# A two-layer decoder stack on one core: late recurrent outputs in the query bank of the next attention, and another order inside a recurrent step

## The chip, the core and the metric

The program runs on one core of a Trainium2 chip. Five engines work from their own instruction queues: TensorE (PE in the profile; its weight loads are the row PEld), VectorE (DVE), ScalarE (ACT), GpSimd (POOL) and SyncE (SP), which here only issues DMAs. An engine runs its instructions in the order in which they were written; engines wait for each other by semaphores. The metric is the device time of one execution in microseconds (us), and the median of several runs is compared.

## The reference

The input x has 2 sequences of 1024 rows and 256 columns, ctx two sequences of 154 rows and 192 columns, all float32. Six blocks are added to x one after the other, each on the layer norm of x:

```
x = x + L0_attn(norm(x)); x = x + L0_xattn(norm(x), ctx); x = x + L0_ffn(norm(x))
x = x + L1_attn(norm(x))          # the recurrent attention
x = x + L1_xattn(norm(x), ctx)    # 16 heads of 16 columns over 154 keys
x = x + L1_ffn(norm(x))           # 8 experts, the best 2 of each row
```

The change is about the fourth block and the beginning of the fifth. In the fourth, `bitlinear(x, w)` is an rms norm of the row, a rounding to integers by the row's largest value, and a product with weights of -1, 0 and 1:

```
i, f, g = bitlinear(x, w_i), sigmoid(bitlinear(x, w_f)), bitlinear(x, w_g)
h[n] = f[n] * h[n-1] + (1 - f[n]) * i[n]              # along the sequence
out  = bitlinear(rmsnorm(h) * g * sigmoid(g), w_o)
```

The fifth is an ordinary attention: queries `norm(x) @ Wq + bq`, softmax over the 154 keys for each of 16 heads, and an output product.

## The kernel before, in words

The 2048 rows are 16 tiles of 128 rows (`NT`); a pair is two tiles (`PAIR`), and there are 8.

**The recurrent stage** is `recurrent`. Each engine runs a loop over `STEPS = NT + LAG` = 29 steps k. In step k TensorE turns the rounded rows of tile k+1 (`turn`), multiplies those of tile k by the three gate weights (`products`), turns forget gate and new state of tile k-1 so that rows lie along the free axis (`scan_turn`), and turns the scanned state of tile k-2 back (`turn_back`). ScalarE makes the sigmoids, the copies and the sums of squares. VectorE scans (L2035, one scan for each half of the columns), multiplies the state that was turned back with the gate (`u`, L2022), makes the gate (L2042) and the new state (L2047), and in `ROW_STEPS` does the row work for tiles 8 to 15 (largest values, scales). GpSimd makes `1 - f` (`keep`, L1791), the gate times its norm (L1785), `zo` = u times its norm (L1796), and the rounding. The rounding of `zo` needs the scale of the row; these scales are made for many tiles at once (`out_scales`, at steps 10 and 18). The output of tile o (turn, copy, product, addition to x at L2052, statistics for the next layer norm at L133) runs in step o + 13, so that steps 16 to 28 hold no new gates, only outputs.

**The cross attention** is the class `CrossNarrow`. Some of it runs inside the recurrent steps, by `pool_step`, `tensor_step` and their like: its keys and values, the split of its weights into a high and a low part (L3464 to L3471, steps 15 to 17), the normalised tiles 0 to 3 (L3476, steps 19 and 20), and the queries of pair 0 (steps 21 to 24). The rest is `run`. There a tile goes through six groups of scores (L3801), their largest values (L3964), the exponentials (L3910), five turns of the probabilities (L3817, L3821; the fifth gets its rest from GpSimd's gather, L3781), the weighing of the values (L3835, L3838), and the output product (L3862). The queries of a pair go through the normalised rows (`normal`), their turn (`turn_x`, L3532), a high part (`high_x`, L3597) and a low part (`low_x`, L3627), 12 products (L3544), a high part (L3608) and a low part (L3634), and 12 DMAs that lay them out by heads (L3433: eight of `cn_qh`, four of `cn_ql`). The scores of a pair's first tile wait for these DMAs.

The order of all this on each engine is fixed before by `order`: a list of work items with an estimated span and the items they depend on is put in a sequence, always taking next the item that could start first by these estimates. The engines then run their part of that sequence.

## Time and profile before

| | |
|---|---|
| median of 3 runs | 1428.05 us (1425.85 to 1431.0) |
| the profiled execution | 1432.4 us, its span 1430.7 us |
| PE, PEld busy | 1296.7 us (91%), 1037.2 us (72%) |
| DVE busy | 1010.1 us (71%) |
| ACT busy | 882.9 us (62%) |
| POOL busy | 457.0 us (32%) |

The shares are means over six blocks with different limits. The profile gives times from the start of the span; the recurrent stage's first gate product starts at 818.38 us and the attention's first scores at 917.25 us. The granted clock is the share of TensorE's full 2.4 GHz that it was allowed in a stretch: 0.50 is 1.2 GHz. A wait is put down to the engine and the line that released it.

### The profile page before, as it was taken

To read this page: it belongs to the slowest core of one execution; us is meant where nothing else is said; L and a number is where in the kernel's file an instruction comes from. 1 tells how busy PE (TensorE), PEld (TensorE's weight loads), DVE (VectorE), ACT (ScalarE), POOL (GpSimd) and SP (SyncE) were. 2 spreads that over 40 slices of the span, in tenths; PEclk is the share of its full clock that TensorE was granted. 3 is DMA by queue.
4 is the path that set the end of the run, shared out by engine and by line. 5 is a ranking of instruction groups with operands and counts; after the bars stand their busy time and mean duration, and the time that the engine had idled before them with its cause. 6 is when DMAs were issued, how large, how long until landed. Compare 5 with 4: busy or idle time off the path is not lost. (4 is left out here: it accounts for less than half of the span.)

```text
span 1430.7 us, 27678 instructions
## 1 busy us (share of the span) xinstructions
PE 1296.7 (91%) x9691; PEld 1037.2 (72%) x9691; DVE 1010.1 (71%) x2014; ACT 882.9 (62%) x2215; POOL 457.0 (32%) x628
## 2 busy tenths in 40 slices
PE   4979999999699999989999866689988699999997
PEld 3534444436599999977888654578877699999995
DVE  4687878734566665556788687578875688888773
ACT  4427666774476666645121467478873688888883
POOL 5311222218444333326000356311100244444430
PEclk8979999999899999999999987599998799999998
DMA  4655422200000000003000210022203577777755
GB/s 91 189 122 138 68 46 47 47 1 5 30 2 2 1 2 1 2 6 121 1 0 1 75 24 1 23 62 47 51 10 107 187 232 232 232 233 233 230 158 188
DMA packets 97916, 116.15 MB, mean 81 GB/s; under 512 B 23549, under 2 KB 83187, under 8 KB 97779
## 3 DMA queue, kind: packets, MB, share of 16 engines
q1 hardware_dynamic: 88323, 99.83, 25.7%
q0 software_dynamic: 4416, 12.06, 2.6%
q10 hardware_dynamic: 5040, 2.49, 0.7%
q8 instruction: 78, 1.28, 0.4%
q14 instruction: 59, 0.48, 0.1%
HBM read 88.47 MB, written 16.55 MB: 73 GB/s over the span
## 5 line engine op out<-in xcount | busy, mean ns | idle before, releaser
L827 ACT ACTIVATE sa_probs<-ps 128x512 f32<-128x512 f32 (+1 forms) x304 | 154.5, 577 | 87.6 <-PE ps L780 86.4
L851 DVE TENSOR_REDUCE sa_top<-ps 128x2 f32<-128x1024 f32 (+3 forms) x160 | 171.8, 1114 | 40.9 <-PE ps L756 25.5
L2738 PE MATMUL ps<-me_h,me_w_parts 128*128 128x256 f32 x1104 | 140.9, 288 | 4.8 <-issue 2.9
L2738 PEld LDWEIGHTS ps<-me_h,me_w_parts 128*128 128x128 f32 x1104 | 137.3, 193 | 6.4 <-issue 3.1
L2752 PE MATMUL ps<-me_w_parts,me_mid 128*128 128x256 f32 x1104 | 136.3, 283 | 0.0
L2752 PEld LDWEIGHTS ps<-me_w_parts,me_mid 128*128 128x128 f32 x1104 | 132.4, 188 | 0.0
L3246 ACT ACTIVATE room<-ps,cx_top 128x154 f32<-128x154 f32 x256 | 96.6, 391 | 35.4 <-DVE cx_top L3295 34.9
L2819 DVE TENSOR_TENSOR me_w_parts<-me_chunk,me_w_parts 128x1024 fp32r<-128x1024 f32 x92 | 110.4, 1222 | 9.9 <-ACT me_w_parts L2779 8.3
L2803 ACT ACTIVATE me_full<-ps,me_b 128x256 f32<-128x256 f32 x184 | 95.2, 518 | 34.7 <-PE ps L2738 34.5
L2849 DVE TENSOR_TENSOR me_mid<-me_full,me_mid 128x256 fp32r<-128x256 f32 x184 | 89.9, 506 | 34.7 <-ACT me_mid L2805 34.6
L3125 POOL TENSOR_TENSOR room<-room 128x512 f32<-128x512 f32 x64 | 67.1, 1049 | 140.7 <-DVE room L3303 140.6
L753 PE MATMUL ps<-sa_k,sa_q 96*128 96x512 bf16 (+3 forms) x384 | 99.1, 342 | 4.8 <-DVE sa_top L851 3.3
L2697 POOL DMA_INDIRECT moe_results<-me_result,mp_target x46 | 53.0, 1151 | 155.5 <-DVE me_result L2837 149.1
L2779 ACT ACTIVATE me_w_parts<-me_chunk 128x1024 fp32r<-128x1024 f32 x92 | 100.1, 1148 | 0.0
L2805 ACT ACTIVATE me_mid<-ps,me_b 128x256 fp32r<-128x256 f32 x184 | 96.4, 524 | 0.0
L1498 PE MATMUL ps<-f_w_high,f_hid 128*128 128x512 f32 (+1 forms) x320 | 91.5, 371 | 2.0 <-DVE x L1660 2.0
L3295 DVE TENSOR_REDUCE cx_top<-ps 128x2 f32<-128x308 f32 x128 | 59.7, 470 | 46.7 <-PE ps L3165 46.0
L780 PE MATMUL ps<-sa_q,sa_k 99*128 99x512 bf16 (+3 forms) x384 | 89.4, 333 | 1.5 <-DMA sa_q<-sa_neg 0.9
L3910 ACT ACTIVATE cn_p<-ps,cn_top 128x154 f32<-128x154 f32 x256 | 79.1, 409 | 7.6 <-DVE cn_top L3964 7.4
L794 PE MATMUL ps<-sa_probs,v_all 128*32 128x512 f32 (+3 forms) x768 | 81.6, 498 | 1.8 <-ACT sa_o_raw L834 1.1
L753 PEld LDWEIGHTS ps<-sa_k,sa_q 96*128 96x128 bf16 x384 | 35.1, 100 | 62.8 <-DVE sa_top L851 32.5
L724 POOL TENSOR_SCALAR_AFFINE_SELECT sa_probs<-sa_probs 128x512 f32<-128x512 f32 x64 | 40.8, 637 | 103.2 <-ACT sa_probs L827 101.6
(466 smaller groups left out, 3370.5 us busy)
## 6 DMA issues: line engine op xcount, KB each, us to landing
me_chunk<-in_L_ffn_W_dram SPq DMA_DIRECT2D x92, 512.0 KB, 4.1
sa_k<-scr_k SPq DMA_DIRECT2D x48, 128.0 KB, 4.5
sa_q<-scr_q SPq DMA_DIRECT2D x96, 64.0 KB, 4.7
cn_qd<-cn_qh SPq DMA_DIRECT2D x60, 64.0 KB, 2.0
scr_q<-room SPq DMA_DIRECT2D x6, 512.0 KB, 5.6
scr_k<-room SPq DMA_DIRECT2D x6, 512.0 KB, 5.8
me_b<-in_L_ffn_b_dram SPq DMA_DIRECT2D x23, 128.0 KB, 3.6
x<-in_x_dram SPq DMA_DIRECT2D x4, 512.0 KB, 6.0
```

The lines of the kernel that those rows point to most:

```text
L753: last = pe.matmul(out[:, a:a + w], self.q_st[0:96, slot, half, h0 + j, q0:q0 + P], self.k_st[0:96, slot, h0 + j, k0:k0 + w], start=True, ...
L827: act.activation(probs[:, step % self.PROBS, h0:h0 + many, 0:w], src[:, :, 0:w], ACT.Exp, scale=DH ** -0.5).then_inc(exped.sem, 1)
L851: dve.tensor_reduce(top2[:, k % 2, k0 // 512, h0:h0 + many, sb % HBLK], src[:, :, 0:w], AX.X, ALU.max).then_inc(freed.sem, 1)
L1498: last = pe.matmul(ps[:, O_BANK + n % RING, 0:w], hid[:, g % 2, net, m, part, cols], wt[:, m, w0:w0 + w], start=(i == 0), stop=(i == len(t ...
L2738: last = pe.matmul(ps[:, MID + n % 4, 0:RT], w[:, u % 2, 0, i, DM * k + P * b:DM * k + P * b + P], h[:, u % 2, j, k, :], start=(m == 0), s ...
L2752: last = pe.matmul(ps[:, OUT + n % 2, 0:D], mid[:, u % 2, b, i, P * a:P * a + P], w[:, u % 2, 1, j, D * b:D * b + D], start=(m == 0), stop ...
L2779: act.activation(part(n, 0), chunk[:, n % BUF, :], ACT.Copy).then_inc(w_high.sem, 1)
L2803: act.activation(full[:, n % 4, :], ps[:, MID + n % 4, 0:RT], ACT.Relu, bias=col).then_inc(s_full.sem, 1)
L2805: act.activation(mid[:, u % 2, b, 0, :], ps[:, MID + n % 4, 0:RT], ACT.Relu, bias=col).then_inc(high.sem, 1)
L2819: dve.tensor_tensor(part(n, 1), chunk[:, n % BUF, :], raw(part(n, 0)), ALU.subtract).then_inc(w_low.sem, 1)
L2849: dve.tensor_tensor(mid[:, u % 2, b, 1, :], full[:, n % 4, :], raw(mid[:, u % 2, b, 0, :]), ALU.subtract).then_inc(low.sem, 1)
L3246: last = act.activation(p[:, h + i, :], ps[:, S_BANK + n % SR, M * i:M * i + M], ACT.Exp, bias=top[:, t % 2, h + i:h + i + 1], accum_out=d ...
```

## The change

It has two parts.

*Inside a step.* VectorE's step is now gate, new state, an output's addition, scan, u, and then the row work. TensorE's is products, scan turns, turn back. On ScalarE the square of the state that was turned back stands behind the copy of the turned forget gate. On GpSimd keep comes first in a step, then the rounding, the gate of the same step, and zo. The split of the attention's weights moves from steps 15 to 17 to steps 2 to 4.

*Late outputs.* The loop has 19 steps (`STEPS = NT + 3`), in which outputs 0 to 5 run (`EARLY`), and three more (`TAIL`) for the queries of pair 0; a normalised pair is now computed at step 17. Outputs 6 to 15 run inside the attention, in the PSUM bank of its queries (`Q_BANK`): 6 to 9 behind the queries of pair 1, 10 to 13 behind those of pair 2, 14 and 15 behind those of pair 3 (`WINDOWS`). GpSimd rounds them (`o_round`), TensorE turns them, ScalarE copies, TensorE multiplies, VectorE adds and makes the statistics. The turn of the next pair waits for the last output of the window before it, since both use the bank. The reciprocal roots of their variances are computed on GpSimd in two parts (`o_rstd`, tiles 6 to 9 and 10 to 15), by a chain of 17 small operations, each of which waits for the one before; the first part stands behind the gather of tile 2, the second behind that of tile 4. Tiles 2 and 3 are now normalised by VectorE in the attention. `order` gets all these items, so its sequence changes.

The core of the diff:

```diff
-    STEPS = NT + LAG
+    STEPS = NT + 3
+    EARLY = STEPS - LAG
...
-        u, zo = sb("u", [P, 2, D]), sb("zo", [P, NT, D])
+        u, zo = sb("u", [P, 2, D]), nx.zo
...
-                for k in range(STEPS):
-                    if 0 <= k - 1 < NT:
-                        at(pool, "gate", k)
-                        pool.tensor_tensor(gate[:, (k - 1) % 4, :], gate[:, (k - 1) % 4, :], norm_g[:, :], ALU.mult
-                                           ).then_inc(s["gated"].sem, 1)
+                pool.tensor_copy(nx.w_o[:, :, :], wt[:, 3, :, :]).then_inc(s["kept"].sem, 1)
+                pool.tensor_copy(nx.magic[:, :], magic[:, :]).then_inc(s["kept"].sem, 1)
+                for k in range(STEPS + nx.TAIL):
                     if k < NT:
                         at(pool, "forget", k + 1)
                         if k >= 2:
                             at(pool, "new", k - 1)
                         pool.tensor_scalar(keep[:, k % 2, :], forget[:, k % 2, :], -1.0, 1.0, ALU.mult, ALU.add
                                            ).then_inc(s["keep"].sem, 1)
+                    if KNOWN <= k + 3 < NT:
+                        rounds(k + 3)
+                    if k < NT:
+                        at(pool, "gate", k + 1)
+                        pool.tensor_tensor(gate[:, k % 4, :], gate[:, k % 4, :], norm_g[:, :], ALU.mult
+                                           ).then_inc(s["gated"].sem, 1)
                     if 0 <= k - 2 < NT:
...
-                    if k + 3 >= LAG and k + 3 < STEPS:
+                    if 0 <= k + 3 - LAG < EARLY:
...
-                for k in range(STEPS):
+                for k in range(STEPS + nx.TAIL):
                     if k + 1 < STEPS:
                         turn(k + 1)
                     nx.tensor_wait(pe, k)
+                    if k < STEPS:
+                        products(k)
+                    if 0 <= k - 1 < NT:
+                        scan_turn(k - 1)
                     if 0 <= k - 2 < NT:
                         turn_back(k - 2)
-                    products(k)
-                    if 0 <= k - 1 < NT:
-                        scan_turn(k - 1)
...
-                for k in range(STEPS):
-                    if 0 <= k - 2 < NT:
-                        t = k - 2
-                        at(act, "back", t + 1)
-                        if t >= 1:
-                            at(act, "sq_h", t)
-                        act.activation(junk[:, 0, 0:D], back_out(t), ACT.Square, accum_out=sum_h[:, t:t + 1]
-                                       ).then_inc(s["sq_h"].sem, 1)
+                for k in range(STEPS + nx.TAIL):
...
-                for k in range(STEPS):
-                    if k in ROW_STEPS:
-                        t = KNOWN + ROW_STEPS.index(k)
-                        rows(t)
-                        if t % 2:
-                            scales(t - 1)
+                for k in range(STEPS + nx.TAIL):
+                    if k < NT:
+                        at(dve, "sig_g", k + 1)
+                        if k >= 4:
+                            at(dve, "u", k - 3)
+                        dve.scalar_tensor_tensor(gate[:, k % 4, :], ps[:, GO, 0:D], unit[:, k, 2:3], sig_g[:, k % 2, :],
+                                                 ALU.mult, ALU.mult).then_inc(s["gate"].sem, 1)
+                        at(dve, "keep", k + 1)
+                        if k >= 2:
+                            at(dve, "s_turned", k - 1)
+                        dve.scalar_tensor_tensor(new[:, k % 2, :], ps[:, FI + k % 2, D:2 * D], unit[:, k, 0:1],
+                                                 keep[:, k % 2, :], ALU.mult, ALU.mult).then_inc(s["new"].sem, 1)
+                    if LAG <= k < STEPS:
+                        o = k - LAG
+                        at(dve, "mm_o", o + 1)
+                        dve.scalar_tensor_tensor(c.x[:, o, :], ps[:, GO, D:2 * D], unit_o[:, o:o + 1], c.x[:, o, :],
+                                                 ALU.mult, ALU.add).then_inc(s["added"].sem, 1)
+                    if 0 <= k - 1 < NT:
+                        t = k - 1
+                        at(dve, "forget_t", t + 1)
+                        if t:
+                            at(dve, "scanned", KD * t)
+                        for d in range(KD):
+                            first = 0.0 if t % ST == 0 else h[:, d, P * t - 1:P * t]
+                            dve.tensor_tensor_scan(h[:, d, P * t:P * t + P], forget_t[:, t % 2, P * d:P * d + P],
+                                                   ps[:, SCAN + t % 2, KD * P + P * d:KD * P + P * d + P],
+                                                   first, ALU.mult, ALU.add).then_inc(s["scanned"].sem, 1)
...
-                    if 0 <= k - 1 < NT:
...
-                    if k < NT:
...
+                    if k in ROW_STEPS:
...
+    TAIL = 3
+    KEPT = NT - 10
+    WINDOWS = {1: range(6, 10), 2: range(10, 14), 3: range(14, 16)}
+    PARTS = ((6, 10), (10, 16))
...
-        if k in (19, 20):
+        if k == 17:
             self.wait(pool, "inverted", 1)
-            for t in (2 * k - 38, 2 * k - 37):
+            for t in (0, 1):
                 pool.tensor_scalar(self.xn[:, t, :], c.x[:, t, :], c.rowstat.mv[:, t, 0:1], self.rstd[:, t:t + 1],
...
-        if k == 21:
+        if k == 18:
             self.turn_x(pe, 0)
-        if k in (22, 23):
-            self.queries(pe, 0, k - 22)
+        if k == 19:
+            self.queries(pe, 0, 0)
+            self.queries(pe, 0, 1)
...
+        if g - 1 in self.WINDOWS:
+            self.wait(pe, "o_add", self.WINDOWS[g - 1][-1] + 1 - self.KEPT)
...
+    def o_round(self, pool, o):
+        pool.tensor_scalar(self.zo[:, o, :], self.zo[:, o, :], self.times_o[:, o:o + 1], ROUND, ALU.mult, ALU.add
+                           ).then_inc(self.s["o_round"].sem, 1)
+    def o_turn(self, pe, o):
+        n = o - self.KEPT
+        self.wait(pe, "o_round", n + 1)
+        for g, tiles in self.WINDOWS.items():
+            if o == tiles[0]:
+                self.wait(pe, "ql", g + 1)
+        if n:
+            self.wait(pe, "o_add", n)
+        for d in range(KD):
+            last = pe.transpose(self.c.ps[:, self.Q_BANK, P * d:P * d + P], self.zo[:, o, P * d:P * d + P], self.c.ident[:, :])
+        last.then_inc(self.s["o_turn"].sem, 1)
+    def o_evict(self, act, o):
+        n = o - self.KEPT
+        self.wait(act, "o_turn", n + 1)
+        act.activation(self.qt[:, :], self.c.ps[:, self.Q_BANK, 0:D], ACT.Identity, bias=self.magic[:, 1:2]
+                       ).then_inc(self.s["o_evict"].sem, 1)
+    def o_product(self, pe, o):
+        self.wait(pe, "o_evict", o - self.KEPT + 1)
+        for d in range(KD):
+            last = pe.matmul(self.c.ps[:, self.Q_BANK, D:2 * D], self.qt[:, P * d:P * d + P], self.w_o[:, d, :],
+                             start=(d == 0), stop=(d == KD - 1))
+        last.then_inc(self.s["o_product"].sem, 1)
+    def o_add(self, dve, o):
+        n, s, x = o - self.KEPT, self.s, self.c.x[:, o, :]
+        self.wait(dve, "o_product", n + 1)
+        dve.scalar_tensor_tensor(x, self.c.ps[:, self.Q_BANK, D:2 * D], self.unit_o[:, o:o + 1], x, ALU.mult, ALU.add
+                                 ).then_inc(s["o_add"].sem, 1)
+        self.wait(dve, "o_add", n + 1)
+        if n >= 2:
+            self.wait(dve, "o_mean", n - 1)
+        dve.bn_stats(self.o_stats[:, n % 2, :], x).then_inc(s["o_seen"].sem, 1)
+        self.wait(dve, "o_seen", n + 1)
+        dve.bn_aggr(self.c.rowstat.mv[:, o, :], self.o_stats[:, n % 2, :]).then_inc(s["o_mean"].sem, 1)
+    def o_var(self, dve, i):
+        a, s = slice(*self.PARTS[i]), self.s
+        self.wait(dve, "o_mean", self.PARTS[i][1] - self.KEPT)
+        dve.tensor_scalar(self.ve[:, a], self.c.rowstat.mv[:, a, 1], EPS, None, ALU.add).then_inc(s["o_var"].sem, 1)
+        self.wait(dve, "o_var", i + 1)
+        dve.tensor_scalar(self.half[:, a], self.ve[:, a].bitcast(I32), 1, None, ALU.arith_shift_right).then_inc(s["o_half"].sem, 1)
+    def o_rstd(self, pool, i):
+        a, s, link = slice(*self.PARTS[i]), self.s, self.o_link
+        v, y, w = self.ve[:, a], self.guess[:, a], self.work[:, a]
+        def then(instruction):
+            instruction.then_inc(link.sem, 1)
+            pool.wait_ge(link.sem, link.next())
+        self.wait(pool, "o_half", i + 1)
+        then(pool.tensor_scalar(y.bitcast(I32), self.half[:, a], -1.0, float(0x5f3759df), ALU.mult, ALU.add))
+        for n in range(4):
+            then(pool.tensor_tensor(w, y, y, ALU.mult))
+            then(pool.tensor_tensor(w, w, v, ALU.mult))
+            then(pool.tensor_scalar(w, w, -0.5, 1.5, ALU.mult, ALU.add))
+            if n < 3:
+                then(pool.tensor_tensor(y, y, w, ALU.mult))
+        pool.tensor_tensor(self.rstd[:, a], y, w, ALU.mult).then_inc(s["inverted"].sem, 1)
...
+            if t in (2, 4):
+                add(("o_rstd", t // 2 - 1, 0), "POOL", 3.5, [("gather", t, 0), ("o_var", t // 2 - 1, 0)])
...
-            if t >= 4:
-                add(("normal", t, 0), "DVE", 0.36, [("turn_x", t // 2 - 2, 0)] if t >= 6 else [])
+            if t >= 2:
+                add(("normal", t, 0), "DVE", 0.36, ([("turn_x", t // 2 - 2, 0)] if t >= 6 else [])
...
-            add(("turn_x", g, 0), "PE", 0.42, [("normal", t, 0) for t in (2 * g, 2 * g + 1) if t >= 4]
-                + ([("low_q", g - 1, 0)] if g > 1 else []))
+            add(("turn_x", g, 0), "PE", 0.42, [("normal", t, 0) for t in (2 * g, 2 * g + 1)]
+                + ([("low_q", g - 1, 0)] if g > 1 else [])
+                + ([("o_add", self.WINDOWS[g - 1][-1], 0)] if g - 1 in self.WINDOWS else []))
...
+                for o in self.WINDOWS[1]:
+                    self.o_round(pool, o)
...
+                    if t < 2:
+                        for o in self.WINDOWS[t + 2]:
+                            self.o_round(pool, o)
+                    if t in (2, 4):
+                        self.o_rstd(pool, t // 2 - 1)
...
+                        for i, part in enumerate(self.PARTS):
+                            if t == part[0]:
+                                self.wait(dve, "inverted", i + 3)
```

The first place where the order changes is TensorE's queue around the query products of pair 1, lines L3544 before and L3564 after; `cn_qd` are the queries, `cn_p` the exponentials. Before:

```order
L3801 MATMUL ps<-cn_kd,cn_qd 128x308 x3
L3801 MATMUL ps<-cn_kd,cn_qd 128x154 x2
L3801 MATMUL ps<-cn_kd,cn_qd 128x308
L3817 MATMUL ps<-ident,cn_p 128x128 x4
L3801 MATMUL ps<-cn_kd,cn_qd 128x308
L3817 MATMUL ps<-ident,cn_p 128x128 x4
L3801 MATMUL ps<-cn_kd,cn_qd 128x308
L3801 MATMUL ps<-cn_kd,cn_qd 128x154
L3544 MATMUL ps<-cn_xh,cn_wqh 128x256
```

After:

```order
L3948 MATMUL ps<-cn_pt,cn_vm 32x128 x16
L3951 MATMUL ps<-cn_pt,cn_vr 128x128 x4
L3914 MATMUL ps<-cn_kd,cn_qd 128x308
L3930 MATMUL ps<-ident,cn_p 128x128 x8
L3962 MATMUL ps<-ident,cn_oraw 128x128 x4
L3930 MATMUL ps<-ident,cn_p 128x128 x8
L3968 MATMUL ps<-ident,cn_on 128x128 x2
L3934 MATMUL ps<-ident,cn_rest 128x128 x4
L3564 MATMUL ps<-cn_xh,cn_wqh 128x256
```

Before, two of tile 0's five turns stood ahead of these products; now tile 0's weighing and all five turns of tile 1 do.

The second place is the same queue around the query products of pair 2 (`cn_pt` are the turned probabilities, `cn_oh` and `cn_ol` the parts of a tile's result). Before:

```order
L3817 MATMUL ps<-ident,cn_p 128x128 x8
L3849 MATMUL ps<-ident,cn_oraw 128x128 x4
L3532 MATMUL ps<-ident,cn_xn 128x128 x4
L3817 MATMUL ps<-ident,cn_p 128x128 x8
L3855 MATMUL ps<-ident,cn_on 128x128 x2
L3821 MATMUL ps<-ident,cn_rest 128x128 x4
L3544 MATMUL ps<-cn_xh,cn_wqh 128x256
```

After:

```order
L3968 MATMUL ps<-ident,cn_on 128x128 x2
L3934 MATMUL ps<-ident,cn_rest 128x128 x4
L3975 MATMUL ps<-cn_woh,cn_oh 128x256
L3975 MATMUL ps<-cn_woh,cn_ol 128x256
L3975 MATMUL ps<-cn_wol,cn_oh 128x256
L3975 MATMUL ps<-cn_woh,cn_oh 128x256
L3975 MATMUL ps<-cn_woh,cn_ol 128x256
L3975 MATMUL ps<-cn_wol,cn_oh 128x256
L3948 MATMUL ps<-cn_pt,cn_vm 32x128 x16
L3951 MATMUL ps<-cn_pt,cn_vr 128x128 x4
L3564 MATMUL ps<-cn_xh,cn_wqh 128x256
```

Before, these were the turns of tile 1, so that the products of pair 2 stood in front of tile 2's scores; now they are the last turns and the weighing of tile 3, and the products stand right behind that weighing.

The third place is VectorE's queue in a recurrent step that also adds an output to x. Before:

```order
L2022 TENSOR_TENSOR hg_u<-ps,hg_gate 128x256
L2026 TENSOR_REDUCE hg_top_o<-hg_zo 128x1
L2035 SCALAR_TENSOR_TENSOR room<-hg_forget_t,room,ps 128x128 x2
L2042 SCALAR_TENSOR_TENSOR hg_gate<-ps,hg_unit,room 128x256
L2047 SCALAR_TENSOR_TENSOR room<-ps,hg_unit,room 128x256
L2052 SCALAR_TENSOR_TENSOR x<-ps,hg_unit_o,x 128x256
```

After:

```order
L2019 SCALAR_TENSOR_TENSOR hg_gate<-ps,hg_unit,room 128x256
L2024 SCALAR_TENSOR_TENSOR room<-ps,hg_unit,room 128x256
L2029 SCALAR_TENSOR_TENSOR x<-ps,cn_unit_o,x 128x256
L2038 SCALAR_TENSOR_TENSOR room<-hg_forget_t,room,ps 128x128 x2
L2048 TENSOR_TENSOR hg_u<-ps,hg_gate 128x256
L2052 TENSOR_REDUCE hg_top_o<-cn_zo 128x1
```

Gate and new state moved from behind the scan to the step's front, and u from in front of the scan to behind it.

## Rows read from the trace of the kernel before

**Rows 1.** Busy time by stretch: us, busy time by engine, clock, DMA share, GB/s

```profile
818.38:886.00 67.62, 43.62 (x268) 34.02 (x268) 56.31 (x136) 48.34 (x133) 37.93 (x68) 0.86 0.11 23
886.00:917.25 31.25, 20.16 (x76) 12.19 (x76) 19.18 (x71) 11.43 (x31) 15.14 (x21) 0.55 0.11 26
917.25:943.31 26.06, 21.86 (x184) 19.37 (x185) 17.34 (x37) 16.94 (x47) 4.02 (x6) 0.79 0.14 31
943.31:956.66 13.35, 11.51 (x108) 9.82 (x109) 11.14 (x24) 11.26 (x35) 1.22 (x2) 1.00 0.35 84
956.66:974.00 17.34, 16.29 (x184) 15.09 (x182) 15.21 (x37) 14.53 (x44) 4.43 (x15) 1.00 0.21 48
974.00:991.35 17.35, 16.31 (x183) 15.11 (x181) 15.20 (x37) 14.53 (x44) 2.44 (x4) 1.00 0.21 47
```

**Rows 2.** Waits of VectorE from 818 to 886: total us, times, longest

```profile
DVE room L2035 <- ACT hg_forget_t L1933: 8.4, 8, 1.3
DVE hg_u L2022 <- ACT hg_junk L1912: 1.6, 5, 0.5
```

**Rows 3.** Timeline of one recurrent step: start, us, engine line

```profile
840.30 0.84 DVE L2035 TENSOR_TENSOR_SCAN room<-hg_forget_t,room,ps 128x128 f32<-128x128 f32 x2
...
842.18 0.43 DVE L2022 TENSOR_TENSOR hg_u<-ps,hg_gate 128x256 f32<-128x256 f32 x1 [0.27 <-ACT hg_junk L1912]
...
843.55 0.40 ACT L1933 ACTIVATE hg_forget_t<-ps 128x256 f32<-128x256 f32 x1
...
843.98 0.85 DVE L2035 TENSOR_TENSOR_SCAN room<-hg_forget_t,room,ps 128x128 f32<-128x128 f32 x2 [1.05 <-ACT hg_forget_t L1933]
```

**Rows 4.** Timeline of the attention's tiles 0 and 1

```profile
920.81 3.42 ACT L3910 ACTIVATE cn_p<-ps,cn_top 128x154 f32<-128x154 f32 x11
...
925.64 0.50 PE L3544 MATMUL ps<-cn_xh,cn_wqh 128*128 128x256 f32 x1
...
933.29 0.86 ACT L3608 ACTIVATE cn_qh<-ps,cn_bq 128x256 fp32r<-128x256 f32 x2
...
934.17 5.12 SPq L3433 DMA_DIRECT2D cn_qd<-cn_qh  x8
...
935.59 0.66 ACT L3910 ACTIVATE cn_p<-ps,cn_top 128x154 f32<-128x154 f32 x2
...
939.35 2.52 SPq L3433 DMA_DIRECT2D cn_qd<-cn_ql  x4
...
943.31 0.48 PE L3801 MATMUL ps<-cn_kd,cn_qd 96*128 96x308 f32 x2 [0.25 <-DMA cn_qd<-cn_ql]
```

**Rows 5.** Stretches of the 12 query products, pairs 1 and 2: PE, PEld, clock

```profile
925.64:928.29 2.65, 2.65 (x12) 2.55 (x12) 0.50 0.00 0
938.57:940.20 1.63, 1.63 (x12) 1.47 (x12) 1.00 0.46 108
```

**Rows 6.** GpSimd's groups by line: busy us, mean ns, idle before, releaser

```profile
L1796 POOL TENSOR_TENSOR hg_zo<-hg_u,hg_norm_o 128x256 f32<-128x256 f32 x16 | 11.6, 726 | 10.4 <-DVE hg_u L2022 10.4
...
L1791 POOL TENSOR_SCALAR room<-room 128x256 f32<-128x256 f32 x16 | 6.5, 406 | 17.9 <-ACT room L1921 17.9
...
L3467 POOL TENSOR_TENSOR cn_wol<-cn_wo,cn_woh 128x512 fp32r<-128x512 f32 x1 | 1.3, 1267 | 0.0
...
L713 POOL TENSOR_SCALAR sa_minus_top<-sa_top 128x16 f32<-128x16 f32 x16 | 4.1, 255 | 99.4 <-issue 79.1 <-DVE sa_top L851 15.8 <-DVE sa_top L856 3.9
```

**Rows 7.** Timeline of the stretch between the last gates and the first scores

```profile
897.34 2.43 POOL L3476 TENSOR_SCALAR cn_xn<-x,x_mv,cn_rstd 128x256 f32<-128x256 f32 x2
...
910.59 2.51 SPq L3433 DMA_DIRECT2D cn_qd<-cn_ql  x4
```

**Rows 8.** DMA issues: count, KB each, us from issue to landing

```profile
cn_qd<-cn_ql SPq DMA_DIRECT2D x32, 64.0 KB, 2.0
```

**Rows 9.** Timeline: the addition of an output to x

```profile
893.33 0.48 DVE L2052 SCALAR_TENSOR_TENSOR x<-ps,hg_unit_o,x 128x256 f32<-128x256 f32 x1
```

**Rows 10.** Two stretches of 4 us inside tiles 0 and 1, columns of rows 1

```profile
920.00:924.00 4.00, 2.10 (x9) 1.84 (x9) 2.97 (x7) 3.87 (x12) 0.00 (x0) 0.50 0.00 0
936.00:940.00 4.00, 3.40 (x26) 2.93 (x27) 3.41 (x9) 1.61 (x4) 1.27 (x2) 1.00 0.45 102
```

137 lines of the change are left out of this document (79 added, 58 removed).

## The prediction

> **What bounds the kernel now.** I read the busy time by stretch first, because the two stages that the change touches are a small part of the span and the page's chain of waits only reaches back to 1089 us. The stretches [rows 1] cut the span at places that can be named in both kernels: the first and the last gate product of the recurrent steps (818.38, 886.00), the first scores of the attention (917.25), and the first scores of its tiles 2, 4, 6 and 8 (943.31, 956.66, 974.00, 991.35). In the recurrent steps VectorE is the busiest engine, 56.31 of 67.62 us. In the 31.25 us behind them nothing is full (TensorE 20.16 at a mean clock of 0.55, VectorE 19.18): that is a chain of short steps for ten more outputs, beside the first queries. From tile 4 on, a pair of tiles takes 17.34 and 17.35 us, in the second of them TensorE is busy 16.31, VectorE 15.20, ScalarE 14.53: a filled pipeline, which has no room for a wait.
>
> The waits inside the recurrent steps show what the reordering is aimed at: VectorE's scan waits for ScalarE's copy of the turned forget gate, 8.4 us in 8 waits, and its product u for ScalarE's square, 1.6 us [rows 2]. One step without new rows shows the loop [rows 3]: scan 840.30, then on TensorE the turn back, on ScalarE its square, the eviction, two sigmoids and, at 843.55, the copy, and the next scan at 843.98, 3.68 us later. All of ScalarE's step stands between two scans.
>
> The attention shows what hides the queries. A pair's queries are 12 products, then copies of high and low parts, then 12 DMAs from one queue. For pair 1 the products start at 925.64, in the middle of tile 0, the DMA issues run 934.17 to 941.87 and the scores of tile 2 start at 943.31, the stall of 0.25 us ending with that DMA [rows 4, 5]. So from the first issue to the scores it is 9.14 us: 7.7 of issuing and about 1.5 from the last issue's end. Pair 2's products start at 938.57, 18 us ahead of the scores that need them (956.66) [rows 5, 1]: that DMA time is hidden, and so it is for every later pair.
>
> **The change part by part.**
>
> *Steps of the recurrence.* The order puts gate, new state and scan ahead of u and the row work on VectorE, and turn back behind the scan turns on TensorE. This breaks the loop above: up to 8.4 + 1.6 = 10.0 us of waits can go [rows 2]. What is late next: in a step without new rows, u (0.43) must reach GpSimd's product (0.73) and then its keep (0.41) before the next new state [rows 3, 6]; with hops that is 2.85 us between u and u against 2.25 of VectorE's own work, so about 0.65 us waits in each of steps 3, 6, 9 and 12. The weight split, moved to steps 2 to 4, puts 1.27 us [rows 6] ahead of one keep in a step that has no row work to cover it. And the first row work, which before lay in the wait for the first gates, now stands behind them: 2.4 us. Sum 2.6 + 1.3 + 2.4 = 6.3, and some 0.7 in the steps that also add outputs: 7, so 3 us of the 10 are saved. Bounds: 0 and 10.
>
> *The end of the stage.* Ten outputs leave it; the chain of the first queries stays. Before, it had three pieces: 11.34 us from the last gate (886.00) to the first normalised tile on GpSimd (897.34), 17.76 from there until the last copy of pair 0 has landed (910.59 + 2.51 + 2.0), and 2.15 to the first scores, in which the last outputs ended [rows 1, 7, 8]. After: the first normalised tile follows the reciprocal of step 17, and I count 3.3 and 2.7 for steps 15 and 16, 1.7 for root, square and u, and 1.4 for the remaining sums and hops, 9.1; the second piece loses about 1 us in front of the low part, which stood behind additions, and 1 us of the outputs between the products; the third goes. 2.2 + 2.1 + 2.2 = 6.5 saved. Bounds: 2.5 if only the third goes, and 10.5 if the 12 products and the turns also run at the high clock (the products in 1.63 instead of 2.65 [rows 5]) and the steps lose no time at the root. The first scores start 9.5 us earlier (3 + 6.5), at about 907.8; bounds 2.5 and 20.5. The four DMAs on ScalarE's queue move from step 24 to 19 with their part; nothing that is awaited is queued behind them. The copies of the output weights and the constant on GpSimd hide in its wait for the first forget gate.
>
> *Pair 1 in the attention.* Normalising tiles 2 and 3 moves into the attention, and in the new order the products of pair 1 stand behind all of tile 1's turns, no longer inside tile 0 (the order of TensorE in the section on the change). Before, tile 1's last exponentials ended at 936.25, 19.0 us after the first scores [rows 4, 1]. After: 2.0 less since the first exponential no longer waits for the roots and the table load (920.81), 2.6 less without the 12 products in front of tile 0's third turn, 0.9 less without the high part, 1.5 more for tile 0's weighing at the low clock: 15.0. Behind it one copy, the high and the low part, 3.6 with hops; products 1.6 [rows 5]; high part 0.86 [rows 4]; 9.14 to the scores: 30.2 against 26.06. Lost 4.1. Bounds 2.4 (clock back before the weighing) and 5.
>
> *Pair 2.* Its turn shares a bank with outputs 6 to 9 and waits for them, and its products now stand behind the weighing of tile 3. From the scores of tile 2: 7.5 us to the end of tile 2's exponentials (1.2 to the first, 16 at 0.31 [rows 4], 0.9 for two copies), output 9 and its statistics to 10, the variance of outputs 6 to 9 at 12.2. Then GpSimd computes the reciprocal root in 17 dependent small operations; the nearest row is 0.26 [rows 6], with a hop 0.31: 5.2, to 17.4. That is a new wait on two engines: tile 3's gather is queued behind the chain on GpSimd, and on VectorE the low output of tile 2 and the last copy of tile 3 behind the first tile that needs the root. So the gather ends at 18.0; then the turn 0.5, its copy 0.7, two normalised tiles and the low part 1.4, the weighing to 21.3, products 1.6, high part 0.9, and 9.14: 33.0 us against 13.35. Lost 19.6. Bounds: without the GpSimd chain in the way 28, so 14.6; with operations of 0.4 each 34.5, so 21.
>
> *Pair 3.* The products stand behind tile 5's turns: 14.5 to the last exponentials, 2.7 for copy, high and low part, 1.6, 0.9, 9.14: 28.8 against 17.34. Lost 11.4. Bounds 9 (no stall among the exponentials) and 13.
>
> *Given back.* Pair 4's products follow at once, so the scores of tile 8 wait for nothing, and at tile 6 less old work is left (queries 4, two turns and an output are done): about 3 us of 17.35 come back; bounds 1.5 and 4. From tile 7 on both orders are the same, so nothing else changes. The ten outputs themselves, on VectorE ten additions of 0.48 [rows 9] and about as much again for their statistics, on TensorE and ScalarE less, run in the three waits and cost nothing; without the waits they would cost up to some 10 us.
>
> Sum: -9.5 + 4.1 + 19.6 + 11.4 - 3.0 = +22.6 us on the profiled execution's 1432.4, which lies 4.35 above the median of 1428.05; carried over to the median, 1450.6.
>
> **The clock in the new waits.** Tile 0 began at a granted clock of 0.50, that is 1.2 GHz, with TensorE busy 2.10 of 4 us; at 936 to 940, with 3.40 of 4 us busy, the clock was at 1.00 [rows 10]. In the new waits TensorE has some 4.5 us of work in 10, which is nearer to the first row. If the clock falls there, each wait is followed by a weighing and 12 products at 1.2 GHz, about 1.5 us more for each (the products took 2.65 us at a clock of 0.50 and 1.63 at 1.00 [rows 5]): 3 times 3 us, +31.6 in all, 1460. No row decides it, since no wait shown is as empty. The Trainium skill (TensorE: Matmul & The Clock Gate, section "HAM oscillation — how this bites in real kernels") says that matmuls in bursts, with longer waits for a transfer between them, start each burst at the slow clock. By that rule it would be the second of the rivals below; by the row at 936 it would not.
>
> **The rivals.**
> 1. Forecast, three exposed query transfers: 1450.6, chance 0.60. For it: engines run their orders in sequence, and the DMA time of 9.14 us is measured.
> 2. The same with the clock lost in each wait: 1460, chance 0.16.
> 3. The waits at their low ends (GpSimd's chain off the path): -9.5 + 2.4 + 14.6 + 9 - 4 = +12.5, 1440.6, chance 0.14. Against it: the gather is queued behind that chain.
> 4. The other side, one mechanism: the recurrent stage gives back all its idle time. All 10.0 us of waits vanish and the end chain runs at the high clock (10.5), so the first scores start 20.5 us earlier; with the waits at their low ends (+22) it is +1.5, 1429.6, no change that can be told. It decides from first scores at 897 on; only before 892 would it be faster. Against it: GpSimd's loop and the clock of 0.55 [rows 1, 6]. Chance 0.07.
> 5. The reordering does not do what it says, TensorE or GpSimd binding the step at 3.7 as before: the start moves by 2.5 to 5 only, +28, 1456, chance 0.03.
>
> **How the numbers follow.** About 0.3% (4.3 us) is what a measurement can tell from no change. Cases 1, 2, 3 and 5 are slower by more than that, 0.93, from which I take 0.03 for what I have not seen: slower 0.90, same 0.06, faster 0.04. The range reaches from below case 3 to above case 2: 1438 to 1463.
>
> **What would show it.** Right: the first scores near 908; TensorE idle in front of the scores of tiles 2, 4 and 6 until the DMA into cn_qd, about 6 to 9 us each; 28 us or more from tile 2's scores to tile 4's, and from tile 4's to tile 6's; the pace of 17.35 per pair from tile 8 on. VectorE's waits for the forget copy near zero. Wrong: tiles 4 and 6 starting 13 to 18 us after the pair before, or first scores before 897.

## The result, and the profile after

| | median, us | lowest to highest | profiled span, us |
|---|---|---|---|
| before (4 runs) | 1427.26 | 1425.85 to 1431.0 | 1430.7 |
| after (4 runs) | 1461.63 | 1457.91 to 1463.35 | 1461.6 |

The ratio of after to before is 1.0233, with a 95% interval of 1.0204 to 1.0262: slower by 33 us (34.4 between the two medians). The forecast was 1450.6 in a range of 1438 to 1463; direction and range held, the likeliest value lies 11 us low.

The stretches of [rows 1] in the changed kernel, with the same columns: first to last gate product, to the first scores, and then from the first scores of tiles 0, 2, 4 and 6 to those of the pair behind:

```profile
816.07:882.89 66.82, 43.41 (x266) 31.44 (x266) 53.93 (x131) 49.08 (x131) 42.60 (x66) 0.82 0.11 23
882.89:906.80 23.91, 9.04 (x38) 6.21 (x38) 12.69 (x45) 7.34 (x23) 7.69 (x11) 0.63 0.13 33
906.80:935.91 29.11, 23.19 (x188) 19.26 (x188) 18.30 (x40) 17.21 (x47) 7.90 (x16) 0.83 0.11 28
935.91:971.48 35.57, 23.56 (x199) 18.86 (x199) 22.52 (x54) 17.25 (x48) 8.04 (x32) 0.85 0.13 32
971.48:1002.41 30.93, 24.18 (x154) 19.81 (x155) 18.12 (x41) 15.93 (x45) 3.52 (x16) 0.72 0.11 26
1002.41:1020.91 18.50, 17.13 (x153) 15.36 (x153) 14.32 (x32) 12.72 (x37) 3.52 (x7) 0.74 0.18 43
```

Against 67.62, 31.25, 26.06, 13.35, 17.34 and 17.35 of [rows 1] that is -0.80, -7.34, +3.05, +22.22, +13.59 and +1.15, together +31.9. The rest of the 30.9 between the two spans is where the first gate product lies (816.07 against 818.38) and 1.3 behind tile 8. The first gate lies between 815.3 and 820.5 in the traces of the changed kernel and of its variants, whose code up to there is the same, so its place can't be put down to an edit; what follows is read between named places of one trace.

What TensorE waited for in front of the scores and the query products, its answer for 905 to 1010 us (total us, times, longest):

```profile
PE ps L3914 <- DMA cn_qd<-cn_ql: 13.0, 3, 6.5
PE ps L3657 <- DVE x L3676: 3.3, 4, 1.2
...
PE ps L3934 <- POOL cn_rest L3889: 2.5, 2, 2.1
PE ps L3564 <- DVE cn_xl L3712: 2.1, 2, 1.4
```

The 6.5 is pair 0's, in front of the first scores of all. And the timeline of pairs 1 to 3, the rows that answer to [rows 4]:

```profile
924.27 0.39 PE L3564 MATMUL ps<-cn_xh,cn_wqh 128*128 128x256 f32 x1
...
926.86 5.06 SPq L3450 DMA_DIRECT2D cn_qd<-cn_qh  x8
...
935.91 0.91 PE L3914 MATMUL ps<-cn_kd,cn_qd 96*128 96x308 f32 x5 [2.39 <-DMA cn_qd<-cn_ql]
...
948.82 0.20 POOL L3701 TENSOR_SCALAR cn_guess<-cn_half 128x4 int32<-128x4 int32 x1 [4.54 <-DVE cn_half L3690]
...
953.36 0.20 POOL L3708 TENSOR_TENSOR cn_rstd<-cn_guess,cn_work 128x4 f32<-128x4 f32 x1
...
958.35 0.36 PE L3564 MATMUL ps<-cn_xh,cn_wqh 128*128 128x256 f32 x1
...
960.92 6.56 SPq L3450 DMA_DIRECT2D cn_qd<-cn_qh  x8
...
971.48 0.76 PE L3914 MATMUL ps<-cn_kd,cn_qd 96*128 96x308 f32 x2 [4.10 <-DMA cn_qd<-cn_ql]
...
991.86 5.06 SPq L3450 DMA_DIRECT2D cn_qd<-cn_qh  x8
996.96 2.51 SPq L3450 DMA_DIRECT2D cn_qd<-cn_ql  x4
...
999.69 0.58 PE L3564 MATMUL ps<-cn_xh,cn_wqh 128*128 128x256 f32 x1 [1.41 <-DVE cn_xl L3712]
...
1002.41 1.40 PE L3914 MATMUL ps<-cn_kd,cn_qd 96*128 96x308 f32 x5
...
1004.23 1.09 PE L3934 MATMUL ps<-ident,cn_rest 128*128 128x128 f32 x4 [0.41 <-POOL cn_rest L3889]
...
1006.19 1.94 PE L3948 MATMUL ps<-cn_pt,cn_vm 128*32 128x128 f32 x32 [0.49 <-DVE cn_pt L4089]
```

Pair 2 reads as the forecast had it: 17 operations on GpSimd in a chain from 948.82 to 953.56 (0.28 each with its hop), the products at 958.35 behind tile 3's weighing, DMA issues from 960.92, scores at 971.48. TensorE's own wait for the DMA is only 4.10 us there, since outputs fill a part of the 10.56 us between the first issue and the scores. Of these 10.56, some 1.4 lie in the issuing: the eight copies took 6.56 us here, 5.06 for pairs 1 and 3, and 5.09 at this place in e2_clock, e5_root and e9_noout, so this is no part of the change. At pair 3 the issues end at 999.47 and the products of pair 4 (999.69) stand in front of tile 6's scores, so that TensorE shows no wait for the DMA there.

The clock in three pieces of 4 us, as [rows 10] (the third column from the end):

```profile
936.00:940.00 4.00, 2.96 (x13) 1.79 (x13) 3.48 (x8) 2.65 (x9) 0.00 (x0) 0.62 0.29 76
968.00:972.00 4.00, 0.52 (x2) 0.50 (x2) 0.00 (x0) 0.00 (x0) 0.00 (x0) 0.50 0.33 82
1004.00:1008.00 4.00, 3.28 (x38) 2.76 (x38) 3.75 (x10) 2.95 (x11) 0.82 (x2) 0.50 0.33 82
```

Around the start of each of the three pairs the clock falls to 1.2 GHz (the 0.62 is the mean of 1.00 up to about 937 and 0.50 behind it); from tile 0 on in the kernel before, this was so only up to about 928, within tile 0.

In the recurrent steps VectorE's wait for the forget copy, 8.4 us in [rows 2], is gone. These came instead, by the answers for all engines (818 to 886 us):

```profile
DVE hg_gate L2019 <- ACT room L1924: 7.2, 4, 2.5
...
POOL room L1781 <- DVE hg_unit L1982: 6.8, 2, 5.1
ACT room L1893 <- DVE hg_unit L1982: 6.3, 2, 4.1
...
DVE room L2024 <- POOL room L1791: 4.7, 8, 1.7
```

In the first VectorE's gate waits for ScalarE's sigmoid. The last line is the keep that the forecast named. The two before it were not foreseen: GpSimd and ScalarE wait for the scales of a row tile, which VectorE now makes at the end of its step (in the kernel before, ScalarE waited 0.5 us for them).

### The profile page after: what moved, and what is told of

The parts are those of the page before. It is cut to its first block and busy times, and to the rows that moved or that the text cites. A ratio compares the mean times of both kernels' runs of the same rounds, so it can differ in the third digit from the quotient of the medians.

```text
span 1461.6 us, 27696 instructions
## 1 busy us (share of the span) xinstructions
PE 1307.2 (89%) x9691; PEld 1043.7 (71%) x9691; DVE 1016.0 (70%) x2020; ACT 885.1 (61%) x2215; POOL 466.6 (32%) x662
```

## The experiments

Ten kernels were run. This is what they gave by stretches, in us, read from each trace, and the medians with their ratio to the kernel before on the same chip.

| kernel | gate 0 to 10 | gate 10 to 15 | gate 15 to first scores | scores of tile 0 to tile 8 | median | ratio (95%) |
|---|---|---|---|---|---|---|
| before | 44.53 | 23.09 | 31.3 | 74.1 | 1427.26 to 1430.21 by chip | 1 |
| after | 40.63 | 26.19 | 23.9 | 114.1 | 1461.63 | 1.0233 (1.0204 to 1.0262) |
| e1_steps | 38.86 | 26.21 | 33.1 | 73.1 | 1431.88 | 1.0015 (0.9996 to 1.0034) |
| e2_clock | 40.63 | 26.41 | 23.9 | 110.0 | 1462.15 | 1.0215 (1.0180 to 1.0251) |
| e3_urge | 40.61 | 26.36 | 26.5 | 104.1 | 1462.25 | 1.0229 (1.0199 to 1.0260) |
| e5_root | 40.62 | 26.18 | 24.0 | 107.6 | 1458.04 | 1.0198 (1.0167 to 1.0230) |
| e9_noout | 40.64 | 26.36 | 24.0 | 106.8 | 1456.55 | 1.0194 (1.0159 to 1.0229) |
| e6_order | 40.62 | 26.19 | 23.9 | 83.3 | 1428.62 | 0.9986 (0.9970 to 1.0001) |
| e7_both | 40.66 | 22.02 | 24.0 | 83.6 | 1425.22 | 0.9970 (0.9953 to 0.9987) |
| e8_rows | 39.99 | 22.02 | 33.4 | 73.9 | 1429.26 | 0.9988 (0.9968 to 1.0007) |
| e10_late | 40.64 | 22.00 | 24.0 | 82.3 | 1423.04 | 0.9956 (0.9941 to 0.9972) |
| e11_early | 39.99 | 22.01 | 34.1 | 67.3 | 1419.86 | 0.9931 (0.9916 to 0.9947) |

A stretch whose code is equal mostly agrees within 0.1 to 0.2 us from trace to trace. Two kinds of stretch do not: the first pair of the attention takes 25.0 to 26.1 us in before, e1_steps and e8_rows, whose attention is the same, and the issuing of eight copies of queries takes 5.06 to 6.56 us. Whole executions of one kernel differ by up to 11 us. So stretches tell what an edit did, within these limits, and medians whether it pays.

**e1_steps: the new order inside a step, alone.** The kernel before with the loops' new order only:

```diff
                     nx.tensor_wait(pe, k)
+                    if k < STEPS:
+                        products(k)
+                    if 0 <= k - 1 < NT:
+                        scan_turn(k - 1)
                     if 0 <= k - 2 < NT:
                         turn_back(k - 2)
-                    products(k)
-                    if 0 <= k - 1 < NT:
-                        scan_turn(k - 1)
```

and likewise on the other three engines.

> Only the new order inside a recurrent step (gate, new state, addition, scan, u, row work on VectorE; turn back last on TensorE; square behind the copy on ScalarE; keep first on GpSimd). All 16 outputs stay in the 29 steps, the weight split stays in steps 15 to 17, the attention is as before. Theory (the ledger of the two traces: last gate product 3.1 us earlier, by the steps alone): about 3 us less than before, 1424, and the stretch behind the last gate as long as before. Rival 1 (the reordering moves the wait from the forget copy to GpSimd's keep and gives nothing): 1427, no change. Rival 2 (the whole 10 us of VectorE's waits go, and what was seen in the changed kernel was spoilt by the weight split in steps 2 to 4): 1417 to 1419.

```profile
815.93:854.79 38.86, 24.69 (x169) 17.67 (x170) 34.66 (x80) 29.50 (x82) 24.94 (x38) 0.96 0.18 39
854.79:881.00 26.21, 18.02 (x99) 13.85 (x97) 19.09 (x52) 18.32 (x48) 13.80 (x26) 0.74 0.01 2
881.00:914.13 33.13, 19.14 (x78) 12.21 (x79) 21.33 (x75) 12.70 (x35) 17.83 (x26) 0.62 0.11 25
```

Gate 0 to gate 10 (first row) gains 5.7 us, gate 10 to gate 15 (second) loses 3.1, and the tail (third) loses 1.9: 0.7 us of gain in all before the attention starts. The median can't tell it from no change, which is rival 1's number. Its mechanism is a small part only: from 815 to 882 us VectorE waits 1.7 us for keep, and 8.1 for ScalarE's sigmoid behind the first gate. Against after (40.63 in the first stretch) the moved weight split and the copies beside it cost 1.8 us; I had 1.3. So rival 2 is half right on the split and wrong on the sum, and the theory's 3 us do not reach the attention.

**e2_clock: is the low clock behind each wait a part of the loss?** 115 matmuls without use fill TensorE's idle time:

```diff
...
+                def keep_busy(ahead, count):
+                    n = NS * ahead
+                    pe.wait_ge(s_exp.sem, s_exp.at(n - SR + 1))
+                    for _ in range(count):
+                        pe.matmul(ps[:, S_BANK + n % SR, 0:D], self.wqh[:, 0, 0:P], self.wqh[:, 0, :], start=True, stop=True)
...
+                    if (what, t, s) in filler:
+                        keep_busy(*filler[what, t, s])
```

> The changed kernel with 115 more matmuls on TensorE that compute nothing needed: they fill its idle time in the three waits (in front of the scores of tiles 2 and 4, and between the outputs 14 and 15 and the queries of pair 4), in a score bank that is free then. Theory (the low clock behind each wait is part of the loss): the granted clock stays at 1.00 from tile 1 on, tiles 2, 4 and 6 run faster, and the time falls by 7 to 11 us, to 1451 to 1455. Rival (behind a wait VectorE and ScalarE set the pace, so the clock costs little): less than 2 us, 1460 or more.

Pairs 1 to 3 and the one behind, as in the first fence of the result:

```profile
911.52:940.24 28.72, 26.29 (x217) 22.19 (x217) 18.18 (x40) 17.15 (x47) 7.83 (x16) 0.86 0.12 29
940.24:975.17 34.93, 29.40 (x253) 25.04 (x254) 22.31 (x54) 17.21 (x48) 8.02 (x32) 0.95 0.13 33
975.17:1003.16 27.99, 22.56 (x188) 18.60 (x186) 17.95 (x41) 16.58 (x47) 3.20 (x15) 1.00 0.12 30
1003.16:1021.53 18.37, 16.02 (x152) 14.39 (x153) 14.62 (x32) 11.74 (x35) 3.84 (x9) 0.81 0.18 44
```

The clock rises from 0.85 to 0.95 and from 0.72 to 1.00 in the second and third stretch, and the four take 110.0 us instead of 114.1; 2.9 of the 4.1 lie between tiles 4 and 6, and the 0.6 at pair 2 is not clean, since the issuing is 1.5 us shorter there. So the clock has a share in the loss, here about 4 us, between what the theory and the rival gave. It is not the whole share: the clock stayed at 0.86 and 0.81 in the first and last stretch, where the theory had 1.00. The median did not fall (1462.15, the rival's number). Of the profiled execution the trace shows why: from the first gate to the end it takes 639.8 us against 645.5 in after, but its first gate lies 4.5 us later. By the total alone the experiment is inconclusive.

**e3_urge: the queries ahead of their turn.** The planner's preferences were changed, for query work by 1 to 1.5 us and for late outputs by 1 to 1.5:

```diff
-        held = {"queries": 0.3, "high_q": 0.3, "high_x": 0.45, "low_x": 0.15, "raw": -0.3}
+        held = {'queries': -1.5, 'high_q': -1.5, 'high_x': -1.5, 'low_x': -1.5, 'low_q': -1.5, 'turn_x': -1.5, 'normal': -1.0, 'raw': -0.3, 'o_turn': -1.0, 'o_evict': -1.0, 'o_product': -1.0, 'o_add': -1.0, 'o_var': -1.5}
```

> The changed kernel with other preferences in the attention's planner: query work and the late outputs are taken 1 to 1.5 us ahead of their turn. Same work, same windows, same bank; the products of pair 1 come behind tile 0's first scores, those of pair 2 ahead of tile 1's scores. Theory (the loss is the transfer of the queries, uncovered because the products stand too late in TensorE's order): no wait for the DMA into cn_qd in front of tiles 2, 4 and 6 beyond 1 us each, and 1417 to 1432 (the earlier start of 10.4 us kept, the ten outputs costing 0 to 15 where they now delay tiles 0 to 3). Rival (the loss is the outputs and their chain through one bank, which now stand in the way of tiles 0 and 1): 1445 or more.

No scores of tiles 2, 4 and 6 wait for a DMA any more, and yet the time is 1462.25: the rival's number. TensorE's waits (905 to 1010 us) say where a part of it went:

```profile
PE ps L3552 <- DVE cn_xn L4076: 9.3, 2, 7.6
PE ps L3669 <- ACT cn_qt L3663: 6.5, 10, 1.2
```

7.6 us of the first row stand ahead of the first scores of all: pair 1's turn was put in front of them, and they start 26.5 us behind the last gate instead of 23.9. Since an output was always preferred, its turn and its product stand next to each other in TensorE's order, and in front of each of the ten products TensorE waits for ScalarE's copy in between (6.5 us). Outputs 6 to 13 now lie within tiles 0 and 1, so from tile 0 to tile 2 it is 37.97 us. Tiles 2 to 8 take 66.1 us against 48.0 before, and no run takes that apart. This order exchanged one exposed wait for another; it does not settle whether an order exists that exposes neither.

**e5_root: is GpSimd's chain on the path?**

```diff
-        for n in range(4):
+        for n in range(1):
             then(pool.tensor_tensor(w, y, y, ALU.mult))
             then(pool.tensor_tensor(w, w, v, ALU.mult))
             then(pool.tensor_scalar(w, w, -0.5, 1.5, ALU.mult, ALU.add))
-            if n < 3:
-                then(pool.tensor_tensor(y, y, w, ALU.mult))
```

> The changed kernel with one refinement instead of four in the reciprocal root on GpSimd: 5 dependent operations instead of 17 (this leaves out accuracy of the root for tiles 6 to 15). Theory (that chain stands on the path of pair 2, since the gather of tile 3 and the first tile that needs the root wait behind it): 12 operations of 0.285 less, 3.4 us less between the scores of tiles 2 and 4, 0 to 1 more at pair 3: 1457 to 1458. Rival (another wait ends at the same time, the outputs or the exponentials of tile 3): less than 1 us.

Tile 2 to tile 4, and tile 6 to tile 8:

```profile
937.27:969.80 32.53, 24.21 (x198) 18.93 (x199) 21.82 (x54) 17.21 (x48) 5.48 (x20) 0.83 0.14 35
...
1000.62:1015.87 15.25, 14.30 (x154) 12.70 (x153) 13.81 (x32) 12.51 (x37) 1.22 (x2) 0.92 0.22 53
```

The first is 3.04 us shorter than after's 35.57, near the 3.4 expected, but only about half of it comes by the chain. From the timeline of pair 2:

```profile
952.08 0.54 POOL L3887 COPY cn_rest<-cn_p 128x416 f32<-128x416 f32 x1
...
958.08 0.36 PE L3564 MATMUL ps<-cn_xh,cn_wqh 128*128 128x256 f32 x1
...
960.70 5.09 SPq L3450 DMA_DIRECT2D cn_qd<-cn_qh  x8
```

Counted from tile 2's scores, the chain is 3.4 us shorter and tile 3's gather starts 3.45 earlier, but the products only 1.63 (20.81 against 22.44) and the first issue 1.58. The other 1.46 is the issuing of the eight copies, 5.09 against 6.56, which is as short in e2_clock and e9_noout with the whole chain. So the chain is on the path, for 1.6 us, and the rival is half right: other waits end soon behind it.

The second, which I had at 0 to 1, is 3.25 shorter than 18.50. In the changed kernel the second chain runs from 998.22 to 1002.93, tile 5's gather behind it starts at 1003.55, and tile 5's last turn waits 0.41 us for that gather. Here the gather starts before tile 6's scores, and tile 5's weighing 3.20 us behind them instead of 3.78. The other 2.7 us lie behind the start of the weighing, with the clock: it is back at 1.00 some 3 us behind tile 6's scores, in after some 10 us, and the first row of the weighing takes 1.08 us instead of 1.94. So the second chain is on the path too, but its own wait is some 0.6 us; that the clock rises sooner because of it is likely and not shown.

**e9_noout: the same order without the late outputs' work** (their turns, copies, products and additions are left out):

```diff
-                    elif what == "o_turn":
-                        self.o_turn(pe, t)
-                    elif what == "o_product":
-                        self.o_product(pe, t)
+                    elif what in ("o_turn", "o_product"):
+                        pass
```

> The changed kernel in the same order, without the turns, copies, products and additions of outputs 6 to 15 in the attention (this leaves out these outputs; the roots are still computed, from older moments). Theory (uncovered query transfers are the loss, the outputs run in their shadow): the scores of tile 2 still start 27 to 28 us behind those of tile 0, tile 4 behind tile 2 by 27 to 31 (GpSimd's chain no longer waits for output 9), tile 6 behind tile 4 by 27 to 29; the time is 1448 to 1456. Rival (the outputs and their bank are the loss): tiles 4 and 6 follow after less than 22 us each, 1440 or less.

```profile
909.89:938.72 28.83, 22.36 (x180) 18.37 (x180) 17.30 (x37) 16.33 (x45) 7.88 (x16) 0.80 0.12 29
938.72:971.13 32.41, 21.05 (x181) 17.55 (x181) 17.81 (x39) 14.82 (x43) 8.05 (x32) 0.82 0.14 35
971.13:999.60 28.47, 20.42 (x140) 17.86 (x140) 13.95 (x29) 15.41 (x44) 5.77 (x21) 0.79 0.12 29
```

Without any output in the way pairs 1, 2 and 3 still take 28.8, 32.4 and 28.5 us. Of the 40 us that the four pairs lost, 33 remain. The rival falls: it is the order that stretches them. The time, 1456.55, lies just above the 1448 to 1456 expected, and pairs 1 and 2 above their bounds of 28 and 31. (At pair 2 the chain on GpSimd was left in.)

**e6_order: the same work in a searched order.** Each item of the query work and of the outputs got a preference of its own; they were chosen by a random search for the least end by the planner's estimate:

```diff
-            add(("laid", g, 0), "SP", 7.5, [("low_q", g, 0)] + behind)
+            add(("laid", g, 0), "SP", 9.2, [("low_q", g, 0)] + behind)
...
-                    key = start + held.get(item[0], 0.0)
+                    key = start + held.get(item[0] + str(item[1]), held.get(item[0], 0.0))
```

> The changed kernel with the same work and the same three windows, but an order of the attention's items that was searched for: a preference of its own for each item of the query work and of the late outputs, taken so that the planner's own estimate of the end is least, with 9.2 us for laying out a pair's queries (measured) instead of 7.5. By that estimate the attention ends 23.5 us earlier. Theory (the loss is an order in which the query products stand too late and every engine then waits for their transfer): the waits for the DMA into cn_qd vanish, tiles 0, 2, 4, 6 and 8 follow each other by 17 to 24 us, and the time is 1436 to 1448. Rival (the ten outputs cost about 30 us inside the attention in whatever order, as the first reordering seemed to say): 1455 or more.

```profile
908.12:928.82 20.70, 15.69 (x122) 13.40 (x123) 14.14 (x32) 14.65 (x41) 5.76 (x12) 0.77 0.18 44
928.82:949.59 20.77, 18.94 (x196) 16.24 (x194) 18.73 (x47) 15.37 (x45) 6.77 (x23) 1.00 0.20 50
949.59:971.79 22.20, 19.10 (x189) 15.54 (x188) 19.54 (x49) 16.60 (x48) 6.37 (x28) 1.00 0.15 37
971.79:991.45 19.66, 18.03 (x195) 16.48 (x194) 17.81 (x41) 15.46 (x46) 3.99 (x9) 1.00 0.17 41
```

The only wait for `cn_qd` that is left in TensorE's answer is pair 0's (5.8 us), the clock is 1.00 from tile 2 on, and the four pairs take 83.3 us instead of 114.1. The time, 1428.62, is even below the theory's range. So the loss of the change is a matter of order: another one takes back 33 us of 34. The search moved all items of the query work and the outputs, so this run does not say how much of it the late query products alone cost. The outputs now show a price of 9 us in a full pipeline, 83.3 against 74.1 in the order before, about what their earlier start saves.

**e7_both and e8_rows: the row work one step earlier**, with late outputs and without them (e7_both also starts the weight split in step 1):

```diff
-    ROW_STEPS, LAG = (1, 2, 4, 5, 7, 8, 10, 11), 13
+    ROW_STEPS, LAG = (0, 1, 3, 4, 6, 7, 9, 10), 13
```

> As e6_order, and in the recurrent steps the row work one step earlier (steps 0, 1, 3, 4, 6, 7, 9, 10) and the first of the weight split's three operations in step 1 instead of 2. Theory (steps 11 and 12 lose 5 to 6 us because GpSimd and ScalarE wait for the scales of the last rows, which VectorE now makes at the end of a step): from gate product 10 to 15 it is 20 to 23 us instead of 26.2, and the time is 3 to 5 us below e6_order. Rival (those two steps are bound by VectorE's own work): within 1 us of e6_order.

> As e1_steps (the step order alone, all outputs in the recurrent steps), and the row work one step earlier (steps 0, 1, 3, 4, 6, 7, 9, 10). Theory as for e7_both: gate product 10 to 15 takes 3 to 6 us less than the 26.2 of e1_steps, and the time is 3 to 5 us below the kernel before. Rival: no more than 1 us.

Gate 10 to 15 falls from 26.2 to 22.0 in both, and in e8_rows no engine waits for the row tiles' scales in that stretch, so this wait was the cause of the 3.1 us that e1_steps lost there. e7_both is 3.4 us below e6_order by the medians; e8_rows gives back 1.1 in the first ten steps and stays within its error of the kernel before, against the 3 to 5 expected.

**e10_late and e11_early: what the late outputs are worth when both sides have a searched order.** The diff is that of e6_order, with other preferences; e11_early has no late outputs.

> As e7_both (late outputs, searched order, row work one step earlier), with a longer search that also has preferences for the items of the tiles. By the planner's estimate the attention ends 4 us earlier than in e7_both. If the estimate holds: 1420 to 1423. If it is below what the estimate can resolve: as e7_both, 1424 to 1427.

> As e8_rows (all outputs in the recurrent steps, new step order, row work one step earlier), with the same search for an order of the attention, which by the planner's estimate ends 10.4 us earlier than in e8_rows, most of it between the scores of tiles 0 and 2 and at the end. Theory 1 (the late outputs pay by themselves, the order only took away their damage): e11_early stays above e10_late, 1425 or more. Theory 2 (what made the searched kernels faster than the kernel before is the order, which the attention without late outputs can have as well, while these outputs cost in a full pipeline about what they save): 1417 to 1423, no slower than e10_late.

Tiles 0 to 8 of e11_early:

```profile
916.48:934.81 18.33, 15.14 (x129) 13.80 (x127) 13.70 (x31) 15.28 (x43) 2.55 (x6) 0.82 0.20 46
934.81:949.97 15.16, 14.19 (x165) 13.07 (x164) 13.19 (x28) 13.31 (x39) 1.93 (x4) 1.00 0.32 72
949.97:966.84 16.87, 16.06 (x183) 15.12 (x182) 15.47 (x36) 14.74 (x44) 4.46 (x15) 1.00 0.22 49
966.84:983.78 16.94, 16.38 (x183) 15.16 (x182) 16.49 (x39) 14.89 (x44) 2.51 (x4) 1.00 0.21 48
```

e11_early takes 1419.86 (ratio 0.9931), e10_late 1423.04, the upper end of what the estimate promised (its tiles 0 to 8 gain 1.3 us on e7_both where the estimate had 4). Theory 2 holds: the attention without late outputs takes the searched order too, 67.3 us from tile 0 to 8 against 82.3. These 15.0 us are more than the 10.1 us by which its scores start later. A searched order gives 6.8 us even where the change had spoilt nothing (67.3 against 74.1), so not all that e6_order won back had been lost by the change. e11_early is the fastest kernel of the study, 9.5 us under the kernel before on the same chip (1429.39).

## Why the prediction was right, and where not

**The mechanism was right.** The products of pairs 1, 2 and 3 stood too late in TensorE's order, and the layout of the queries was no longer covered. e9_noout keeps 33 of the 40 us without the outputs' work, and e6_order takes 31 of them away with all of it. Of the signs named, the first scores (906.8), 28 us or more for pairs 2 and 3, the 17.35 from tile 8 on and the forget copy came. One did not: TensorE idle for 6 to 9 us in front of each pair's scores. Its last waits for the DMA were 2.39, 4.10 and none, as outputs and the products of pair 4 lay in the transfer's time.

**The step that was mis-sized is "Given back".** I had -3.0 from tile 6 to tile 8; measured is +1.15. I had counted GpSimd's chain of 17 for tile 3 and pair 2, but not the second one for tile 5, which stands in the same way in front of a gather; and I had put the clock there at no cost, though it was at 0.74. With that chain cut short and the clock at 0.92, e5_root gives 3.25 us of the 4.15 back. By its timeline some 0.6 of them are the chain's own wait, and the rest goes with the clock.

**The other terms.** Pair 1: +4.1, measured +3.05. Pair 2: +19.6, measured +22.2. Pair 3: +11.4, measured +13.6, with the queries of pair 4 in front of its scores. At pair 2, 1.4 of the 2.6 between is the longer issuing (10.56 from the first issue to the scores, 9.14 in the forecast); no run settles the rest. At pair 3 the 2.2 between has the size of what e2_clock gave back there, 2.9. The chain on GpSimd took 4.74, forecast 5.2; the price of having it in the way, 5.0 by the bounds, seems put too high: leaving out 12 of its 17 operations moved the products of pair 2 by 1.6 (e5_root).

**The earlier start, -9.5.** Between first gate and first scores it was -8.1, so the sum was near, but partly by luck, since two errors stand against each other: the steps gave 0.8 instead of 3, the end 7.3 instead of 6.5. For the steps I had named keep, weight split and the first row work as what is late next, and missed the last scales (steps 11 and 12), as e8_rows shows.

**"The ten outputs cost nothing in the waits."** Without them the four pairs were 7.3 us shorter (e9_noout), 1.5 of them by the longer issuing at pair 2; the rest fits with the turns of pairs 2 and 3 and the first chain, which wait for the last output of a window. My bound of 10 us for a pipeline without waits depends on the order: 9 in e6_order against the order before, but 15.0 where both sides have a searched order (e10_late and e11_early).

**The rivals.** Rival 2, the clock, was put at 0.16 and 9 us. The clock did fall at each pair: 0.62, 0.50 and 0.50 around the first scores of tiles 2, 4 and 6. The Trainium skill (TensorE: Matmul & The Clock Gate, section "HAM oscillation — how this bites in real kernels") has this for bursts of matmuls with longer waits for a transfer between them, and the trace agrees at tiles 2 and 4; at tile 6 the clock fell at about 995 us, among the short waits of outputs 14 and 15. Its price is 3 to 4 us by e2_clock, which left the stretch behind tile 6 at 0.81, and up to 2.7 more there by e5_root. Rival 2's time, 1460, is nearest to the result. What happened lies between it and the forecast: of the 9.3 us between the forecast sum (+22.6) and the measured one (+31.9) some 3 to 7 are the clock's, 1.4 are the longer issuing, some 0.6 the second chain's own wait, and 1.4 the smaller gain ahead of the attention, with 1.1 to the other side at pair 1. Rival 3 fell by pair 2 (22.2 against its 14.6) and by e5_root (the chain is on the path), rival 4 by the first scores at 906.8, rival 5 because VectorE's wait for the forget copy did go.

What stays open: no run keeps the clock at 1.00 throughout, e2_clock shows its 4 us in the trace and not in its median, and e5_root changes the chain and the clock at once, so how the loss is shared between the two is argued, not shown. No run moves the query products back and nothing else; e3_urge was meant to, and moved the outputs with them.
